# Two chained attention layers on one core: another dealing of a turn's steps, and the low parts of x and h subtracted on VectorE

## The reference

```python
# layer 0
q = Wq @ x + bq            # 32 x N
k = Wk @ x + bk            # 32 x N
v = Wv @ x + bv            # 256 x N
attn = softmax(q.T @ k, axis=-1)
x1 = gamma * (v @ attn.T) + x
# layer 1
h = group_norm(x1, 32 groups, eps=1e-5) * w + b
q, k, v = Wq1 @ h + bq1, Wk1 @ h + bk1, Wv1 @ h + bv1      # 256 x N each
attn = softmax(q.T @ k / 16, axis=-1)
y = x1 + Wp @ (v @ attn.T) + bp
```

## Time and profile before

| | us |
|---|---|
| median of 3 timed executions | 869.07 (867.05 to 870.95) |
| profiled execution | 862.52 |
| its span | 860.7 |
| TensorE busy | 798.7 (93%) |
| VectorE busy | 533.6 (62%) |
| ScalarE busy | 470.6 (55%) |
| GpSimd busy | 202.9 (24%) |
| mean granted TensorE clock | 0.97 |

### The profile page before, as it was taken

The page is one execution under the profiler, slowest core; times in us unless marked ns, Lnnn a source line. Parts: engine busy times, 40 slices in busy tenths (PEclk is TensorE's granted clock), DMA queues, the critical chain, the costliest instruction groups (busy, mean ns, idle before and its releaser), DMA issues.

```text
span 860.7 us, 9679 instructions
## 1 busy us (share of the span) xinstructions
PE 798.7 (93%) x3756; PEld 651.8 (76%) x3756; DVE 533.6 (62%) x765; ACT 470.6 (55%) x609; POOL 202.9 (24%) x163
## 2 busy tenths in 40 slices
PE   5789788989899989999899998999999999999998
PEld 4568666877688767888678886888778877888786
DVE  5554664756557674585666756577755866475565
ACT  4765663548455575545664575554945447444343
POOL 3500251114220161103511035101521015101310
PEclk9889998999899999999899999999999999999999
DMA  7000001001100011000200002000100001000101
GB/s 220 1 0 2 1 1 49 1 1 50 49 1 1 0 50 49 1 1 1 85 14 1 0 1 98 1 2 1 49 1 1 1 1 49 1 1 1 50 1 50
DMA packets 10366, 18.98 MB, mean 22 GB/s; under 512 B 2128, under 2 KB 3920, under 8 KB 10320
## 3 DMA queue, kind: packets, MB, share of 16 engines
q1 hardware_dynamic: 10320, 18.36, 6.1%
HBM read 9.97 MB, written 8.39 MB: 21 GB/s over the span
## 4 chain that ended last, share of the span: by engine, by line
PE 64%; DVE 17%; ACT 15%; issue 3%; DMA 1%; SPq 0%; ACTq 0%; DVEq 0%
PE ring L507 20%; PE ring L509 19%; PE ring L508 19%; ACT prob L724 4%; DVE neg_raw L908 3%; PE ring L517 3%; ACT prob L721 3%; ACT pt_hi L735 3%; DVE pt_lo L923 3%; PE ring L527 2%; DVE bn L966 2%; ACT h_hi L711 2%; DVE neg_max L906 2%; ACT ring L745 1%; ACT pt_hi L738 1%
## 5 line engine op out<-in xcount | busy, mean ns | idle before, releaser
L507 PE MATMUL ring<-pt_hi,v_hi 128*128 128x512 f32 x512 | 203.7, 398 | 3.6 <-DVE x L956 2.0
L508 PE MATMUL ring<-pt_lo,v_hi 128*128 128x512 f32 x512 | 201.7, 394 | 0.0
L509 PE MATMUL ring<-pt_hi,v_lo 128*128 128x512 f32 x512 | 201.5, 394 | 0.0
L724 ACT ACTIVATE prob<-ring,neg_max 128x1024 f32<-128x1024 f32 x64 | 71.6, 1118 | 169.0 <-DVE neg_max L909 169.0
L908 DVE TENSOR_REDUCE neg_raw<-ring 128x1 f32<-128x1024 f32 x64 | 77.9, 1217 | 87.2 <-PE ring L509 87.2
L923 DVE TENSOR_TENSOR pt_lo<-prob,pt_hi 128x1024 fp32r<-128x1024 f32 x64 | 89.8, 1404 | 49.3 <-ACT pt_hi L735 48.9
L507 PEld LDWEIGHTS ring<-pt_hi,v_hi 128*128 128x128 f32 x512 | 97.8, 191 | 25.1 <-issue 4.5
L509 PEld LDWEIGHTS ring<-pt_hi,v_lo 128*128 128x128 f32 x512 | 97.2, 190 | 21.7
L508 PEld LDWEIGHTS ring<-pt_lo,v_hi 128*128 128x128 f32 x512 | 97.8, 191 | 19.0
L906 DVE TENSOR_REDUCE neg_max<-ring 128x1 f32<-128x1024 f32 x64 | 77.7, 1222 | 47.6 <-PE ring L517 47.6
L507 PE MATMUL ring<-h_hi,query_hi 128*128 128x512 f32 x256 | 102.2, 399 | 2.5 <-ACT ring L745 2.1
(11 more groups left out here) (118 smaller groups left out, 1299.9 us busy)
## 6 DMA issues: line engine op xcount, KB each, us to landing
out_y<-res SPq DMA_DIRECT2D x32, 256.0 KB, 2.1
x_in<-in_x SPq DMA_DIRECT2D x7, 1024.0 KB, 4.9
x_in<-in_x SPq DMA_DIRECT2D x2, 512.0 KB, 5.1
h_f<-in_wv_t SPq DMA_DIRECT2D x1, 256.0 KB, 5.2
res<-in_wq SPq DMA_DIRECT2D x1, 256.0 KB, 6.7
res<-in_wk SPq DMA_DIRECT2D x1, 256.0 KB, 6.9
res<-in_wv SPq DMA_DIRECT2D x1, 256.0 KB, 7.4
res<-in_wp_t SPq DMA_DIRECT2D x1, 256.0 KB, 7.2
```

The source lines that it names most:

```text
L507: mm(out, w_hi, m_hi, start=first, stop=False)
L508: mm(out, w_hi, m_lo, start=False, stop=False)
L509: return mm(out, w_lo, m_hi, start=False, stop=last)
L724: activation(prob[:, p % PROBS], ring[:, slot], ACT.Exp, bias=neg_max[:, k % 2:k % 2 + 1], accum_out=row_sum[:, k % 2:k % 2 + 1]).then_inc ...
```

## The change

The plan of the steps is dealt anew. In a turn, qk(i+1, 1) moves from step 2 to step 3, the two query tiles from steps 3 and 4 to 4 and 5, the first three value1 tiles to steps 6 to 8, and the last to the end of step 14. The two small norm results are written into the second bank of the slot that a value0 (or, for image 0, qk) tile holds, instead of taking a slot (HOST, `norm_place`); the next holder of that slot waits for the norm's reader as well. In the opening the score tiles, the logarithm and the shift of images 1 and 2 and the keys of image 1 are placed otherwise. VectorE's order within a step changes: q/k splits come ahead of the tile's pt_lo, and the evacuation of layer 1 is done at the end of the step of the last values, ahead of that step's pt_lo, not at the start of the next.

The low parts: x_lo of images 3 to 7 is subtracted by VectorE at the end of step 14 (in the opening, of the step of logits 6), and ScalarE rounds x_hi in step 13. h_lo of images 1 to 6 is subtracted by VectorE in step 2, both halves; in images 0 and 7 one half stays with GpSimd. x_lo of image 2 stays with GpSimd. The amount of arithmetic is the same.

```diff
--- before.py
+++ after.py
@@ -41,8 +41,8 @@
...
         self.early, self.sides, self.late = [], [], []
-        self.log = self.shifts = self.hidden = self.split_x = None
-        self.statistics = self.evacuate = None
+        self.early_log = self.log = self.shifts = self.hidden = self.hidden_lo = self.split_x = self.split_x_lo = None
+        self.statistics = self.evacuate = self.evacuate_at_once = None
         self.take_weights = False
...
@@ -52,11 +52,17 @@
...
 PLACE.update({("weights", 0, m): 3 for m in range(4)})
-PLACE.update({("value1", i, m): m for i in (0, IMAGES - 1) for m in (2, 3)})
-
-
-X_LO_ON_DVE = (0,)
-H_LO_ON_DVE = (0, IMAGES - 1)
+PLACE.update({("value1", IMAGES - 1, m): m for m in (2, 3)})
+PLACE.update({("value1", 0, 0): 2, ("value1", 0, 1): 3, ("value1", 0, 2): 2, ("scores", 2, 5): 3,
+              ("value1", 0, 3): 2})
+
+
+HOST = {("norm", 0, m): ("qk", 2, m) for m in range(2)}
+HOST.update({("norm", i, m): ("value0", i + 1, 2 + m) for i in range(1, IMAGES - 1) for m in range(2)})
+GUEST = {host: guest for guest, host in HOST.items()}
+
+
+H_LO_HALVES = (0, IMAGES - 1)
 
...
@@ -82,19 +88,23 @@
...
         if k == 2:
-            step.late = tiles("scores", 1, (0, 1))
-        if 3 <= k < TILES:
+            step.late = tiles("scores", 1, (0,))
+        if 3 <= k <= 5:
+            step.early = tiles("scores", 1, (k - 2,))
+        if 6 <= k <= 8:
             step.early = tiles("scores", 1, (k - 1,))
...
     steps[4 + 5].sides = tiles("bias", 0, (0,))
-    steps[4 + 7].late = tiles("scores", 1, (7,))
-    steps[4 + 7].log = steps[4 + 7].shifts = 1
+    steps[4 + 5].late = tiles("scores", 1, (4,))
+    steps[4 + 8].early_log = 1
     steps[4 + 8].sides = tiles("value0", 1, (2,))
     steps[4 + 8].late = tiles("shift", 1, (0,))
-    steps[4 + 9].late = tiles("keys", 1, (0,)) + tiles("value0", 1, (3,)) + tiles("keys", 1, (1,))
-    steps[4 + 9].split_x = 2
+    steps[4 + 9].sides = tiles("keys", 1, (0,))
+    steps[4 + 9].late = tiles("value0", 1, (3,))
+    steps.append(Step(("keys", 1, 1)))
+    steps[-1].split_x = 2
     return steps
...
@@ -110,7 +120,7 @@
...
     s6.sides = tiles("value0", 2, (0,))
-    s6.hidden = 0
+    s6.hidden = s6.hidden_lo = 0
     s7.early = tiles("scores", 2, (1,))
...
@@ -121,18 +131,17 @@
...
     ones = [Step(("logits", 0, k), (1, 0, k - 2) if k >= 2 else None) for k in range(TILES)]
-    ones[0].late = tiles("value1", 0, (2,))
+    ones[0].late = tiles("value1", 0, (2,)) + tiles("scores", 2, (5,))
     ones[1].late = tiles("value1", 0, (3,))
     ones[2].statistics = 1
-    for k, m in ((3, 2), (4, 3)):
-        ones[k].sides = tiles("value0", 2, (m,))
-        ones[k].late = tiles("scores", 2, (k + 2,))
-    ones[4].late = tiles("norm", 1, (0,)) + ones[4].late
-    ones[5].sides = tiles("scores", 2, (7,))
+    ones[3].late = tiles("scores", 2, (6,))
+    ones[4].sides = tiles("value0", 2, (2,))
+    ones[4].late = tiles("norm", 1, (0,)) + tiles("scores", 2, (7,))
+    ones[4].log = ones[5].shifts = 2
+    ones[5].sides = tiles("value0", 2, (3,))
     ones[5].late = tiles("norm", 1, (1,))
-    ones[6].log = ones[6].shifts = 2
-    ones[7].sides = tiles("shift", 2, (0,))
-    ones[6].split_x = 3
+    ones[6].sides = tiles("shift", 2, (0,))
+    ones[5].split_x = ones[6].split_x_lo = 3
     return steps + ones
...
@@ -151,10 +160,9 @@
...
             step.banks_first = 1
-    steps[2].banks_first = 0
     if has(i + 1):
         steps[0].sides = tiles("qk", i + 1, (0,))
-        steps[2].sides = tiles("qk", i + 1, (1,))
+        steps[3].sides = tiles("qk", i + 1, (1,))
         for k, s in enumerate((4, 5, 6, 7)):
...
@@ -164,23 +172,24 @@
...
     if has(i - 1):
-        for m, s in enumerate((3, 4)):
+        for m, s in enumerate((4, 5)):
             steps[s].sides = tiles("query", i - 1, (m,))
-        for m, s in enumerate((5, 6, 7, 8)):
+        for m, s in enumerate((6, 7, 8)):
             steps[s].sides = tiles("value1", i - 1, (m,))
-        steps[1].hidden = i - 1
+        steps[14].late = tiles("value1", i - 1, (3,))
+        steps[1].hidden = steps[2].hidden_lo = i - 1
     if i == IMAGES:
         steps[0].hidden, steps[1].hidden = i - 1, None
-        steps[7].sides = []
+        steps[0].hidden_lo, steps[2].hidden_lo = i - 1, None
+        steps[8].sides, steps[14].late = [], []
         for m, s in ((2, 8), (3, 9)):
-            steps[s].sides = []
             steps[s].late = tiles("value1", i - 1, (m,))
...
     if has(i + 2):
-        steps[14].split_x = i + 2
+        steps[13].split_x, steps[14].split_x_lo = i + 2, i + 2
     return steps
...
@@ -190,6 +199,9 @@
...
         RING_NO[_entry] = len(RING_NO)
+        if _entry in HOST:
+            SLOT[_entry], BEFORE[_entry] = SLOT[HOST[_entry]], None
+            continue
         _slot = PLACE.get(_entry, min(_step.slots, key=_given.get))
...
@@ -203,7 +215,10 @@
...
         if _k == TILES - 1:
-            STEPS[_n + 1].evacuate = (_layer, _image)
+            if _layer == 0:
+                STEPS[_n + 1].evacuate = (_layer, _image)
+            else:
+                _step.evacuate_at_once = (_layer, _image)
 TILE_OF = list(TILE_NO)
...
@@ -325,6 +340,10 @@
...
 
+        def norm_place(entry):
+            first = HALF * (entry in HOST)
+            return ring[:, SLOT[entry], first:first + CT]
+
         S = {name: ctx.enter_context(nc.semaphore(name)) for name in SEMAPHORES}
...
@@ -411,18 +430,17 @@
...
 
-                if i - 1 in H_LO_ON_DVE:
+                if i > 0:
                     pool.wait_ge(S["h_split"], CT * i)
...
             def split_hidden(i):
-                for ct in range(1 if i in H_LO_ON_DVE else CT):
-                    pool.wait_ge(S["h_full"], CT * i + ct + 1)
-                    pool.wait_ge(S["h_hi"], CT * i + ct + 1)
-                    G.tensor_tensor(h_lo[:, ct], h_f[:, ct], h_hi[:, ct].bitcast(F32),
-                                    ALU.subtract).then_inc(S["h_split"], 1)
+
+                pool.wait_ge(S["h_full"], CT * i + 1)
+                pool.wait_ge(S["h_hi"], CT * i + 1)
+                G.tensor_tensor(h_lo[:, 0], h_f[:, 0], h_hi[:, 0].bitcast(F32), ALU.subtract).then_inc(S["h_split"], 1)
 
...
@@ -487,9 +505,8 @@
...
                 hidden(i)
-                if 0 < i < IMAGES - 2:
-                    split_x(i + 2)
-                split_hidden(i)
+                if i in H_LO_HALVES:
+                    split_hidden(i)
                 residual1(i)
...
@@ -591,7 +608,7 @@
...
                     wait("norm_read", 2 * i + 1)
-                return mm(out[:, 0:CT], group_s[:], mean_var[:, :, 0] if m == 0 else spread[:], start=True, stop=True)
+                return mm(out, group_s[:], mean_var[:, :, 0] if m == 0 else spread[:], start=True, stop=True)
 
...
@@ -628,6 +645,8 @@
...
                         wait("key_hi", 2 * before[1] + before[2] + 1)
+                    if before in GUEST:
+                        wait(*reader(GUEST[before]))
                 if kind == "scores":
...
@@ -645,7 +664,7 @@
...
                 elif kind == "norm":
-                    last = group_sums(i, m, out)
+                    last = group_sums(i, m, norm_place(entry))
                 elif kind == "weights":
...
@@ -800,7 +819,11 @@
...
                     follow(now.tile)
-                for entry in now.early + now.sides:
+                for entry in now.early:
+                    follow(entry)
+                if now.early_log is not None:
+                    log_sums(now.early_log)
+                for entry in now.sides:
                     follow(entry)
...
@@ -840,11 +863,11 @@
...
 
-                ct = CT - 1
-                dve.wait_ge(S["h_full"], CT * i + ct + 1)
-                dve.wait_ge(S["h_hi"], CT * i + ct + 1)
-                V.tensor_tensor(h_lo[:, ct], h_f[:, ct], h_hi[:, ct].bitcast(F32),
-                                ALU.subtract).then_inc(S["h_split"], 1)
+                for ct in range(1 if i in H_LO_HALVES else 0, CT):
+                    dve.wait_ge(S["h_full"], CT * i + ct + 1)
+                    dve.wait_ge(S["h_hi"], CT * i + ct + 1)
+                    V.tensor_tensor(h_lo[:, ct], h_f[:, ct], h_hi[:, ct].bitcast(F32),
+                                    ALU.subtract).then_inc(S["h_split"], 1)
 
...
@@ -936,7 +959,7 @@
...
                 dve.wait_ge(S["ring_ready"], RING_NO[entry] + 1)
-                got = ring[:, SLOT[entry], 0:CT]
+                got = norm_place(entry)
                 if m == 0:
...
@@ -991,23 +1014,33 @@
...
                     prob_lo(pending)
+                if now.hidden_lo is not None and now.hidden_lo not in H_LO_HALVES:
+                    split_hidden(now.hidden_lo)
                 for entry in now.early:
                     follow(entry)
+                if now.early_log is not None:
+                    shifts(now.early_log)
+                first = [entry for entry in now.sides if entry[0] == "qk"]
+                for entry in first:
```

(14 more changed lines are left out.)

## The result

The changed kernel takes 839.23 us, the median of 4 runs (836.84 to 842.42); the kernel before, run beside it, 868.06 (860.63 to 870.95). The ratio is 0.9713 (0.9669 to 0.9758). The profiled execution took 842.42, its span 840.6, 20.1 us less than the 860.7 of before. The medians differ by 28.8, so 8.7 of the gain is how other executions stand to the profiled one (the profiled execution of the changed kernel is the slowest of its four). In the four groups of experiments, with 20, 15, 8 and 11 runs, the kernel before had medians of 862.04 to 864.06, and the changed kernel, run again beside 15 of them, gave 0.9752, 21.8 us: the gain is more likely near 22 us than near 29. I explain the 20.1.

A forecast was written before the change was run, and what follows sets the result against it. TensorE, busy 93% of the 860.7 us span, was taken as the bound; -6.6 + 5.6 - 1.1 - 1.0 = -3.1, with the clock's -2.8 together -5.9 from the 869.07 median: 863.2 us, range 849 to 876.

The forecast's parts named there:

- the four turns: Turns of images 3 to 6: stalls of 5.0 us against 3.6 before, +1.4 each, +5.6 us in all.
- the clock: Low-clock stretches after TensorE idles: three falls of 2 us, 6 us, in place of 8.8, so -2.8 us.
- image 2's turn: No value1 tile before x_lo, VectorE idle, only later stalls stay: 2.5 against 3.6 us, -1.1 (-2.2 to +0.5).
- image 7's: Image 7's turn: the earlier evacuation removes the 1.04 us idle at 718.34, -1.0 (0 to -1.5); the end 0.
- the opening: Images 0 and 1: the new dealing shortens or removes TensorE's waits, -6.6 us (-10 to -2).
- The stall at the score tile: First score tile waits for VectorE's second q/k split, 2.1 us a turn, with about 0.6 behind it.
- The stall at q/k: Step 0's q/k projection waits 2.3 us (0 to 3.5) as x_lo, interrupted by v1_lo, delays logits 7's maximum and exponent.
- the clock falls after each new idle: Rival, chance 0.22: low clock twice a turn in images 2 to 6, 18 us against 8.8, giving 875.2 us.
- the dealing brings only a little: Rival, chance 0.19: the opening's waits reappear at the next instruction, gain 1.6 instead of 6.6 us, giving 868.2 us.
- The norm wait: The 0.82 us wait for the norm's reader moves from the score tile to the logits behind it: 0 net.
- x rounded a step sooner: Two ScalarE casts move into a stretch where it waits for logits: 0 us (-0.5 to +1).
- VectorE keeps its turn: Rival, chance 0.19: two VectorE subtractions run uninterrupted, both stalls about 1 us, no clock fall: -22.2, giving 846.9 us.

The follow-up runs named there:

- e7_h_one_more: Changed kernel with only the first half of h_lo of images 1 to 5 subtracted twice on VectorE: 852.52 us, 0.9880 of the kernel before.
- e1_x_early: Changed kernel with VectorE's x_lo in step 14 moved ahead of the value1 tile's read, right behind the reciprocal: 831.21 us, 0.9625 of the kernel before.
- f2_qk_later: Changed kernel with VectorE's q/k splits put back behind the tile's pt_lo: 855.02 us, 0.9920 of the kernel before.
- e5_place: Changed kernel with image 0's value1 tiles and score tile 5 of image 2 in their old PSUM slots: 842.11 us, 0.9753 of the kernel before.
- f1_evac_later: Changed kernel with layer 1's evacuation put back to the start of the next step: 850.07 us, 0.9851 of the kernel before.
- d4_low_only: Kernel before with the low parts (x_lo, h_lo) moved to VectorE and nothing dealt anew: 865.55 us, 1.0025 of the kernel before.
- e2_h_twice: Changed kernel with each half of h_lo of images 1 to 5 subtracted twice on VectorE: 867.55 us, 1.0033 of the kernel before.
- d1_deal_only: Changed kernel with the new dealing kept but the moved x_lo and h_lo subtractions back on GpSimd: 858.42 us, 0.9952 of the kernel before.
- d3_x_dve: Changed kernel with x_lo still on VectorE but h_lo of images 1 to 6 as before on GpSimd: 850.80 us, 0.9856 of the kernel before.

## Why the prediction was wrong

The prediction's sum, made right step by step with the spans, goes from -5.9 to -20.1: the four turns -10.3 (forecast +5.6, measured -4.7), the clock -6.0 (forecast -2.8, the turns' -8.8), image 2's turn -2.4, image 7's -0.6, the opening +5.0 with its own clock in it. The other 10 of the 24.0 us between 863.2 and 839.23 are how the other executions of both kernels stand to the profiled ones.

**The stall at the score tile (forecast 2.1 and 0.6 behind it, measured 0.49 and none) is the step that failed.** VectorE's chain, from the exponent of logits 7 at 496.91 to the split's end at 512.58, is 15.7 us and not 17.0. The 1.1 us "one GpSimd copy in between" was the wrong term: the copy waited instead (3.07 us for 1.2 us of work), and VectorE's subtractions follow at 1.13 (505.65, 506.78), less than the 1.2 I took. TensorE's way to the same tile is 15.4 from that exponent (0.15 of hand-over, then 497.06 to 512.35) and not 14.9. So 1.3 and 0.5 us, on a difference of two sums of 15, turned 2.1 into 0.3 and 0.2 of hand-over. With this stall went the 0.6 behind it. That VectorE's chain decides here, as the prediction put it, is shown by e7_h_one_more, where 1.23 us more in it are 1.26 more of wait.

**The stall at q/k (forecast 2.3, measured 1.66).** The mechanism was right, shown by e1_x_early; the interruption by v1_lo was right too, shown by 3.45 us in four turns against 2.34 for image 2's x_lo, which has no v1_lo beside it. x_lo with v1_lo in it took 3.45 and not 3.75, and v_f was read 0.25 sooner than I put it. A turn's idle is then 1.66 + 0.49 in place of 3.26 and small ones: 98.8 to 99.1 us at full clock against 100.00, -1.2 on the mean where +1.4 stood. So the largest positive term of the sum had the wrong sign.

**The clock (forecast -2.8, measured -8.8 in the turns).** I took three falls of 2 us out of nine idles. There was none in the turns, whose longest idle is 1.68. The rival "the clock falls after each new idle" was wrong for this kernel, but not by its mechanism: with 1.3 us more at the score tile, f2_qk_later shows it in five turns of five. What failed is my use of it: I counted falls among idles of 2.0 to 2.3, and the idles were 1.66 and 0.49. One row I had also misread: behind 186.37 not 12 but some 8 matmuls were slow, about 1.6 us.

**The opening (forecast -6.6, measured -1.6).** The idles of 186.37 and 201.10 went, as forecast (4.3 with the slow matmuls). What was missed is the PLACE line: value1 of image 0 in the slots of the values, which the text of the diff shows, and which made the 4.52 at 146.11. But e5_place says that other waits of the same chain, 5.45 us, stand behind it: a term that removes a wait late in a chain wins nothing if the chain's own length is what ends last. Between 44 and 113 us, waits of 1.98, 2.09, 2.16, 1.64 and 2.26 stand where 3.46, 1.97, 2.26, 2.18 and 1.60 stood: keys waits less and the score tile behind it more. The third rival, "the dealing brings only a little", had its price (-1.6) here. How much of the 5.0 missed is structure and how much the opening's own low clock, which varies by 6.8 us between profiles, stays open.

**Image 2's turn (forecast -1.1, measured -3.5 without the clock).** VectorE is idle there, as said, so there was no stall at q/k, and at the score tile TensorE was idle for 0.18 where the forecast had 2.5, the same error as above.

**Image 7's turn and the end (forecast -1.0, measured -1.6).** The 1.04 of 718.34 went. f1_evac_later has it back and takes 150.2 us for this stretch, 1.3 more than the changed kernel; the other 0.3 I have not traced. **The norm wait** moved to logits at 0.93: right. **x rounded a step sooner**: no ScalarE wait for it in any turn: right.

The rival that came closest was "VectorE keeps its turn", 846.9: its four turns at -0.9 each and its clock at -8.8 stand beside the measured -1.2 and -8.8, and only its opening was much too large. In part that is luck: its condition, that two subtractions of VectorE are not interrupted, held for h_lo and not for x_lo, and it had both stalls at 1 us, where they were 1.66 and 0.49. I had held two rows against each other (2.77 and 1.52) and read one rule, alternation, from them. The Trainium skill, GPSIMD Engine Reference (Key points), was cited as a rule against this change, as GpSimd contends with VectorE's two-input instructions. The trace agrees that they contend (3.45 for 2.35), but not that it decides: GpSimd had 36 us less to do, and of the new subtractions only x_lo's was hit. The Trainium skill, VectorE: DVE Perf Modes (The TRN2 errata), has a formula that gives 1.22 us for one such subtraction, and 4.9 us a turn for the four, an estimate. The trace agrees for one (1.22 for half of h_lo); the four take 2.35 and 3.45, 5.8 us a turn, of which v1_lo is 1.1.

**What stays open**: why the executions of the kernel before scatter more (860.63 to 870.95) than one profile explains; that the low clock follows more of its 3.26 us idles in some is likely, but not shown (four of five did in its trace, and four of five in that of d4_low_only). Also what lets the copy in or not, what the split's order is worth in the opening, and the last 0.3 us a turn of e1_x_early's gain.

## What to carry to other kernels

A wait that an edit shifts should be priced in both sums to a few tenths where it is their difference, and with what the clock adds behind it: in f2_qk_later 1.3 us on VectorE cost 3.5 a turn. Parts of a change are judged together when one moves what another waits for: here -0.5% and +0.3% alone, -2.5 to -2.9% together. Where an operation is ready early and the one behind it waits, as x_lo and the read of value1 here, try it ahead: that one move brought another 9 to 11 us.

## What the runs showed of the hardware

- Who waits, when VectorE and GpSimd both subtract, is not alternation alone. v1_lo (two inputs) got in after one of two VectorE subtractions in 4 of 4 turns; the residual copy (one input) waited out two, 3.06 to 3.07 us; but in e2_h_twice, where a wait on a semaphore stood between VectorE's subtractions, it did get in. Small ones wait too: GpSimd's 128x2 instruction behind v1_lo (L425) took 1.67 us in each of the four turns of images 3 to 6, and 0.69 in d1_deal_only.
- Idles of TensorE within turns and the matmuls at the low level (8 at 0.43 us, some 1.5 us in all, and up to 14 behind the longer idles) behind them: of 1.65 to 1.68 us, behind none of 28 (four each in the changed kernel, its repeat, e5_place, d3_x_dve, f1_evac_later, f2_qk_later and e2_h_twice) and behind one of 4 in e7_h_one_more; of 1.75, behind 2 of 3; of 1.78 to 1.84, behind 5 of 5; of 3.50 to 3.84 in e2_h_twice, behind 5 of 5; of 4.1, behind 8 of 8. But one of 3.20 in the kernel before (525.76) was followed by none, where its four like ones were (3.21 to 3.26), and so was one of 3.24 in d4_low_only (327.70): the length of the idle alone does not decide. In the openings, idles of 2 us and more had them in some profiles, as 8 behind the 2.26 of 112.87 in the changed kernel, and none behind the like 2.25 in e1_x_early. These are single traces: other executions of the same kernels had another mean clock (0.982 to 0.993 in the changed kernel).
